# Attention's order respaced, intermediate rows stored for one batch only, and Q and K loaded in transfers to 48, 32 and 16 partitions

## What is computed

```python
qkv = x @ qkv_w.T                      # rotary positions on q and k
outs.append(_sdpa(q[:, :6], k[:, :6], v[:, :6], 1 / sqrt(16)))
# hyperbolic heads:
inner = einsum('bhtd,bhsd->bhts', q, k) - tq * swapaxes(tk, -1, -2)
arg = maximum(-curv * inner, 1 + 1e-7)
scores = 1 / (eps + sqrt(1 / curv) * arccosh(arg)) + causal_bias
outs.append(softmax(scores) @ v)
outs.append(_sdpa(qn, kn, v[:, 10:], sqrt(16)))
x = layernorm(x + concat(outs) @ proj_w.T + proj_b)
# experts: 1024 tokens x top 2 of 8, on the flattened rows
x = layernorm(x + experts(x) + bias)
```

## Time and profile before

| what | value |
|---|---|
| median of 3 runs | 1947.89 us |
| the profiled execution | 1950.01 us, span 1948.4 us |
| projection, 0 to 276 us of the span | 276 us |
| attention, 8 turns, 276 to 1722 us | about 181 us each |
| experts and end | 226 us |
| busy in the span: TensorE, ScalarE, VectorE, GpSimd | 1608.7, 1393.3, 1203.7, 756.2 us |
| DMA, share of 16 engines | 37.5% for the hardware queue, 5.6% for GpSimd's |

### The profile page before, as it was taken

How to read it: one execution, slowest core, us unless ns; L and a number is a source line. 1 busy time by engine, 2 the same in 40 slices (tenths; PEclk the granted TensorE clock), 3 DMA queues, 4 the chain that set the end, 5 groups by cost and what they waited for, 6 DMA issues and landing times.

```text
span 1948.4 us, 38980 instructions
## 1 busy us (share of the span) xinstructions
PE 1608.7 (83%) x13082; PEld 905.8 (46%) x13082; DVE 1203.7 (62%) x3014; ACT 1393.3 (72%) x1460; POOL 756.2 (39%) x369
## 2 busy tenths in 40 slices
PE   7999937876987898789779977986897789779993
PEld 4655612333443344344334433442443344369992
DVE  6877836634766686577657665765785577532234
ACT  2655638896897889788878987897889788851220
POOL 3344333443433444353435434344433465430003
PEclk9999959988997999899889988998998899779997
DMA  4699850255034405510650254054206511358893
GB/s 156 214 242 282 233 154 12 76 87 89 13 50 84 110 2 89 122 34 2 110 122 13 35 96 114 2 73 112 59 2 110 125 34 51 103 195 279 292 338 100
DMA packets 75777, 215.01 MB, mean 110 GB/s; under 512 B 18064, under 2 KB 27664, under 8 KB 69744
## 3 DMA queue, kind: packets, MB, share of 16 engines
q1 hardware_dynamic: 66400, 179.16, 37.5%
q0 software_dynamic: 9200, 33.43, 5.6%
HBM read 143.95 MB, written 68.58 MB: 109 GB/s over the span
## 4 chain that ended last, share of the span: by engine, by line
PE 33%; issue 14%; DVE 9%; ACT 9%; POOL 7%; DMA 5%; SPq 2%; DVEq 0%; POOLq 0%; ACTq 0%
PE a_o L1214 6%; PE a_w L1259 4%; PE a_s L715 4%; PE a_s L727 4%; PE a_s L1199 4%; POOL a_Z L1487 3%; POOL a_R L1484 3%; DVE a_X L1728 2%; PE a_w L1227 2%; PE a_w L1303 2%; DMA K<-t_parts 2%; ACT a_PT L1396 2%; SPq L1120 2%; DMA x_mid<-a_X 2%; ACT a_Z L1414 2%
## 5 line engine op out<-in xcount | busy, mean ns | idle before, releaser
L1396 ACT ACTIVATE a_PT<-a_s 128x1024 f32<-128x1024 f32 (+3 forms) x576 | 460.0, 810 | 154.3 <-PE a_s L1202 94.1
L1487 POOL TENSOR_TENSOR a_Z<-a_Z,a_R 128x2182 f32<-128x2182 f32 x64 | 290.0, 4531 | 449.0 <-ACT a_R L1408 442.2
L1199 PE MATMUL a_s<-Q,K 96*128 96x512 bf16 (+7 forms) x1152 | 330.7, 352 | 103.7 <-ACT a_PT L1396 75.5
L1484 POOL TENSOR_TENSOR a_R<-a_Z 128x2182 f32<-128x2182 f32 x64 | 245.1, 3830 | 242.1 <-DVE a_Z L1600 206.8
L1608 DVE TENSOR_REDUCE a_mx<-a_w 128x1 f32<-128x512 f32 (+2 forms) x576 | 307.3, 550 | 44.0 <-PE a_w L1227 37.7
L1214 PE MATMUL a_o<-a_PT,a_V 128*32 128x512 f32 (+3 forms) x2304 | 271.0, 545 | 74.8 <-ACT a_PT L1396 47.5
L1600 DVE TENSOR_SCALAR_CACHE_REDUCE a_Z<-a_w 128x512 f32<-128x512 f32 (+7 forms) x384 | 202.8, 528 | 116.8 <-PE a_w L1242 69.6
L1259 PE MATMUL a_w<-a_ident,a_R 128*128 128x128 f32 (+1 forms) x1152 | 202.5, 301 | 37.3 <-DVE a_PTh L1654 22.6
L1654 DVE COPY a_PTh<-a_w 128x512 f32<-128x512 f32 (+1 forms) x256 | 158.2, 622 | 102.0 <-PE a_w L1259 100.0
L1227 PE MATMUL a_w<-K,Q 96*128 96x512 bf16 (+2 forms) x576 | 188.8, 334 | 26.4 <-DVE a_mx L1608 10.1
L1199 PEld LDWEIGHTS a_s<-Q,K 99*128 99x128 bf16 (+1 forms) x1152 | 111.4, 103 | 198.8 <-ACT a_PT L1396 105.7
(11 more groups left out here) (166 smaller groups left out, 2539.9 us busy)
## 6 DMA issues: line engine op xcount, KB each, us to landing
qk_parts<-p_parts SPq DMA_DIRECT2D x128, 192.0 KB, 3.4
Q<-in_w SPq DMA_DIRECT2D x46, 512.0 KB, 6.2
K<-in_w SPq DMA_DIRECT2D x46, 512.0 KB, 7.4
Q<-qk_parts SPq DMA_DIRECT2D x144, 128.0 KB, 5.4
K<-qk_parts SPq DMA_DIRECT2D x144, 128.0 KB, 8.1
v_rows<-p_vt SPq DMA_DIRECT2D x8, 2048.0 KB, 9.7
a_V<-v_rows SPq DMA_DIRECT2D x32, 512.0 KB, 9.8
p_xT<-in_xt SPq DMA_DIRECT2D x8, 1024.0 KB, 8.3
```

The lines of the kernel that those rows point to most:

```text
L1199: m = pe.matmul(sB[x % 2][:, i, 0:w], Kb[0:r, h, P * j:P * j + P], Qb[0:r, h, t0:t0 + w], start=True, stop=not diag)
L1396: act.activation(PT[:, u % 2, 2 * k:2 * k + 2, 0:w], sB[x % 2][:, :, 0:w], ACT.Exp, scale=scale_of(GROUPS[g][2 * k])).then_inc(prob.sem, 1)
L1484: pool.tensor_tensor(r, z, z, ALU.mult).then_inc(z_sq.sem, 1)
L1487: pool.tensor_tensor(z, z, r, ALU.add).then_inc(z_sum.sem, 1)
```

## The change

1. **Transfers.** The six pairs are reordered to Q parts 0, 0, 0, 1, 1, 2 and K parts 0, 1, 2, 0, 1, 0. A run of equal Q parts is one transfer whose source is read three times or twice (stride 0), and the K parts of that run are one transfer over three or two parts. So Q and K have transfers of 48, 32 and 16 partitions: 6 for groups 0 and 2, 12 for group 1, and 12 for group 3, of which 6 carry roots into 3, 2 and 1 partitions. The same bytes are moved.
2. **`mid_out`** is executed for batch 0 only. For that, turn 1 stands before the loop on VectorE and GpSimd (code only). For other batches `add_bias` waits for the first layer norm and not for the store.
3. **Order.** The units' `ready` are (13, 35, 51, 66, 87, 102, 118, 135) and were 12, 29, 46, 64, 81, 99, 116, 134; the arguments stand within 6 to 18 quarter steps ahead of it. In the chain `log_distance` and `inverse` come 1 quarter step later, `row_bias` 2, the exponentials 3, 2, 2 and 3, the transposes 6 and 2. The maxima start one step earlier. The late part is respaced and its second layer norm stands 4 to 5 quarter steps earlier. In the final stretch, where late items are mixed into the experts, all that still wait are taken at the last place of the list.

```diff
-QPART = (0, 0, 1, 0, 2, 1)
-KPART = (0, 1, 0, 2, 0, 1)
+PAIRS = ((3, 0), (2, 1), (1, 2))
...
+    def copies(src, n, first, same):
+        if same:
+            return src[first:first + 1].to_broadcast([n, *src.shape[1:]])
+        return src[0:n]
+
+    for qk, buf in enumerate((Qb, Kb)):
+        r = 0
+        for n, part in PAIRS:
+            src = qk_parts[bass.ds(b, 1), qk, :, 2 * BR * block:2 * BR * (block + 1), :]
+            src = src.rearrange("o s (d h) t -> (o s) d h t", d=HD)
             for h0, h1 in runs:
                 i0 = BLOCKS[block].index(h0)
-                found.append((g, buf, r * HD, (r + 1) * HD, (h0, h1, src[:, i0:i0 + h1 - h0, :])))
+                found.append((g, buf, r * HD, (r + n) * HD,
+                              (h0, h1, copies(src[:, :, i0:i0 + h1 - h0, :], n, part, qk == 0))))
...
+        READY = (13, 35, 51, 66, 87, 102, 118, 135)
+        SPREAD = (7, 3, 1, 2, 2, 1, 2, 2)
+        CHAIN = (('square', 0), ('log_square', 4), ('root', 6), ('add_root', 8), ('log_sum', 13), ('log_distance', 16), ('inverse', 18), ('row_bias', 21))
...
-                         (112, ("newton", 0)), (114, ("normalize", 0, 0)), (115, ("normalize", 0, 1)), (116, ("mid_out",)),
-                         (121, ("add_bias",)), (123, ("statistics", 1, 0, NT // 2)), (124, ("statistics", 1, NT // 2, NT)),
...
                 elif kind == "mid_out":
-                    rows_out(d, x_mid, 0, mid_sent)
+                    if is_routed(d):
+                        rows_out(d, x_mid, 0, mid_sent)
...
                 elif kind == "add_bias":
-                    dve.wait_ge(mid_sent.sem, mid_sent.at(d))
+                    if is_routed(d):
+                        dve.wait_ge(mid_sent.sem, mid_sent.at(d))
+                    else:
+                        dve.wait_ge(normed.sem, normed.at(d, 0))
```

More of the change, by code:

```diff
@@ L32 @@
 GW = P // HD
-QPART = (0, 0, 1, 0, 2, 1)
-KPART = (0, 1, 0, 2, 0, 1)
-NPAIR = len(QPART)
+PAIRS = ((3, 0), (2, 1), (1, 2))
+NPAIR = sum(n for n, _ in PAIRS)
 KR = NPAIR * HD
@@ L598, in head_loads @@
     found, block = [], BLOCK_OF[g]
[L599 to L602, removed]
+    def copies(src, n, first, same):
[7 more added lines that the diff above has]
+            src = src.rearrange("o s (d h) t -> (o s) d h t", d=HD)
             for h0, h1 in runs:
                 i0 = BLOCKS[block].index(h0)
-                found.append((g, buf, r * HD, (r + 1) * HD, (h0, h1, src[:, i0:i0 + h1 - h0, :])))
[L606 to L610, removed]
+                found.append((g, buf, r * HD, (r + n) * HD,
+                              (h0, h1, copies(src[:, :, i0:i0 + h1 - h0, :], n, part, qk == 0))))
+            if g == 3:
+                src = t_parts[bass.ds(b, 1), :, qk * N_HYP:(qk + 1) * N_HYP, :].rearrange("o s h t -> (o s) h t")
+                found.append((g, buf, KR + r, KR + r + n, (HYP0, COS0, copies(src, n, part, qk == 0))))
+            r += n
     return found
@@ L921, in put @@
             work[at // NSLOT][at % NSLOT].append(item)
-        for n in range(NU):
-            ready = LEAD + SPAN * n // (NU - 1)
+        READY = (13, 35, 51, 66, 87, 102, 118, 135)
+        SPREAD = (7, 3, 1, 2, 2, 1, 2, 2)
+        CHAIN = (('square', 0), ('log_square', 4), ('root', 6), ('add_root', 8), ('log_sum', 13), ('log_distance', 16), ('inverse', 18), ('row_bias', 21))
+        for n, ready in enumerate(READY):
             args = [("argument", n, k, pc) for k, seg in enumerate(segments(n)) for pc in range(len(seg[3]))]
-            span = 2 * len(args) if n else 8
+            span = SPREAD[n] * len(args) if n else SPREAD[n]
             for a, item in enumerate(args):
                 put(ready - span + a * span // len(args), item)
[L929 to L939, removed]
+            for kind, at in CHAIN:
+                put(ready + at, (kind, n))
+            for k, at in enumerate((23, 24, 26, 29)):
+                put(ready + at, ("hyp_exp", n, k))
+            for part, at in enumerate((33, 34)):
                 for q in range(len(turns(n, part))):
-                    put(ready + turned + q, ("turn", n, part, q))
+                    put(ready + at + q, ("turn", n, part, q))
             if n % 2:
@@ L959, in columns_of @@
             return hs[0] * NT, (hs[-1] + 1) * NT
[L961 removed]
+        SUMS = {0: 119, 1: 121, 2: 143, 5: 149, 6: 155, 7: 163, 3: 178, 4: 179}
+        ROWS, PROJECT, STATISTICS = (40, 46, 54, 63, 71, 80, 86, 94), (42, 52, 55, 64, 77, 84, 91, 95), (48, 53, 61, 71, 81, 86, 94, 97)
         for n, at in SUMS.items():
             put(at, ("turn_sums", n))
[L964 removed]
+        put(40, ("unstage",))
         for k, n in enumerate(SUMS):
[L966 to L969, removed]
[L970 to L973 removed]
+            put(ROWS[k], ("turn_rows", n))
+            put(PROJECT[k], ("project", n))
+            put(STATISTICS[k], ("statistics", 0, n, n + 1))
+        for at, item in ((25, ("shift",)), (104, ("variance", 0)), (106, ("inverse_root", 0)), (112, ("newton", 0)), (114, ("normalize", 0, 0)), (115, ("normalize", 0, 1)), (116, ("mid_out",)), (117, ("add_bias",)), (118, ("statistics", 1, 0, NT // 2)), (119, ("statistics", 1, NT // 2, NT)), (120, ("variance", 1)), (121, ("inverse_root", 1)), (124, ("newton", 1)), (126, ("normalize", 1, 0)), (128, ("normalize", 1, 1)), (128, ("rows_out",)), (136, ("rows_in",))):
             put(at, item)
@@ L987, in attend, with is_routed @@
                 "rows_out", "shift")
+        def is_routed(d):
+            return isinstance(d, int) and d == 0
         def is_late(item):
@@ L1012, in attend @@
                 finish += [("second", t - 1), ("y_copy", t - 1)]
-            take = SIZES[t] if t < len(SIZES) else 0
+            take = SIZES[t] if t < len(SIZES) - 1 else len(waiting)
             finish, waiting = finish + waiting[:take], waiting[take:]
@@ L1556, in _ @@
             pool.wait_ge(others, 16 * NOTHER)
-            with nc.Fori(1, B - 1, engines=[pool.engine], hint_back_edge=True) as b:
+            turn(1)
+            with nc.Fori(2, B - 1, engines=[pool.engine], hint_back_edge=True) as b:
                 turn(b)
@@ L1769, in _ @@
             dve.wait_ge(others, 16 * NOTHER)
-            with nc.Fori(1, B, engines=[dve.engine], hint_back_edge=True) as b:
+            turn(1)
+            with nc.Fori(2, B, engines=[dve.engine], hint_back_edge=True) as b:
                 turn(b)
```

7 lines of the change are left out of this document (3 added, 4 removed).

## The result

The changed kernel took **2099.27 us** (median of 4 runs, 2087.64 to 2104.90), the kernel before 1948.43 beside it: ratio 1.0751, 95% interval 1.0711 to 1.079. The profiled execution took 2087.64 us. It is slower, as forecast, but by 151 us by the medians (137.6 between the profiled executions) where 58 were forecast, and above the range.

The account below looks back on a forecast made before the run. Attention was taken as bound by TensorE and ScalarE waiting for each other, projection by TensorE. 42 + 47 + 16 - 24 - 9 - 14 = +58 on 1950.0 gave 2008, less 2.1 above the median: 2006 us, range 1930 to 2050.

Parts of the forecast that it names:

- How many engines: Loads of Q and K: transfers to 48 and 32 partitions use 3 and 2 DMA engines, not 16.
- the bracket `<-DMA K<-t_parts`: Sign in the profile after: a wait of about 9 us at the first argument of every turn.
- the four late p_xT: Sign in projection: waits for p_xT, the batch's input, of 5 to 17 us in four batches.
- Projection +42: Projection: loads issued ahead crowd the first engine and delay the next batch's input; +42 us, bounds +21 and +54.
- "28.2 us" from last to first argument: Between turns' arguments: the load of `heads(3)` sets 28.2 us; six stretches, average 20.4 before, give +47, bounds +31 and +62.
- The first transition, "0": First stretch from last to first argument: 28.1 us already, so no change, 0.
- Restart at the low clock +16: Turn after the wait on TensorE: slower after waiting, 6 x 2.7 = +16 us (0 to +32).
- The store -24: Dropped store of x_mid: VectorE's sum with the bias no longer waits for it, -24 us (0 to -24).
- Respacing and the quarter step -23: Attention turn: stretched chain and respacing -14 us (-49 to +14); one quarter step less between first and last argument -9.
- The layer norm beside GpSimd, "0": Layer norm on VectorE: its hold beside GpSimd leaves the first, returns at the second; 0 (-25 to +9).
- Rival A: Loads of Q and K: split over sixteen engines by the 48 partitions written, -71, 1877 us; chance 0.14.
- "1965 to 2045": Whole kernel: span in us given to the forecast case alone, said to span the terms' bounds.

Follow-up runs that it names:

- e6: The changed kernel, with SyncE waiting for the landing of `heads(3)` before it issues `heads(2)`: 2075.63 us.
- e7: The changed kernel, with `out` and the load of X moving one eighth of their bytes from the second turn on: 2070.85 us.
- e9: The changed kernel with both edits, the wait of e6 and the cut of `out` and X of e7: 2036.40 us.
- e1_order: The changed kernel's order and dropped store of x_mid, with the 16-partition transfers of the kernel before: 1965.82 us.
- e5_order_wait: e1_order, with SyncE waiting for the landing of `heads(3)` before it issues `heads(2)`: 1922.28 us.
- e3_sixteen: The changed kernel, same pieces into 48, 32 and 16 partitions, but with the 16 rows of a head as outermost count: 1902.36 us.
- e11: The kernel before, without the store of x_mid in turns 1 to 7 and nothing else changed: 1952.74 us.
- e2: The kernel before, with the changed kernel's new transfers (`PAIRS` and `head_loads`) alone: 2161.37 us.
- e14: The kernel before, with the transfers of e3_sixteen and without the store of x_mid in turns 1 to 7: 1930.67 us.

## Why the prediction was wrong in size

**How many engines: right.** 3 engines for 48 partitions: the share is 19.0% and a row takes 0.34 us. This reading carried the direction. Right too were the bracket `<-DMA K<-t_parts` in every turn and the one x_mid wait left. The bracket was to be about 9 us and was 18. Of the four late p_xT, forecast at 5 to 17 us, two came at 19 and 16 us, one at 4 and one at 0.3.

**Projection +42: right**, +46.

**"28.2 us" from last to first argument: the term that failed.** It was 38.5 in the mean of the last six, and 37.5 in the first turn, where I had written 0. Six were short by 10.3 us each and the first by 9.4: 71 us, which is the whole miss of 69 in this row (my 20.4 for before's six was 20.7). The measured +116 also lies above the upper bound of this term, +62. Its parts, for one of the six stretches, by the runs:
- `heads(2)` beside it: 3.2 us (e6). The sum had nothing for what is issued behind the load.
- `out` and X: 2.7 us for seven eighths of their bytes, thus 3.1 in all (e7), where 2.6 stood for X, and nothing for `out`.
- Both together took off 8.0 (e9, 38.5 to 30.5), 2.1 more than their sum: each seems to hide a part of the other.
- What is left is 30.5 against the 25.6 that my sum gives without X: the row of 0.33 us, taken from one row on a quiet chip, holds only in the calm (0.32); at the start of a load it is 0.45. The first row came 1.5 to 4.5 us after its issue (4.5 behind `out`), not 1, and in e6 and e9 the argument starts 0.6 us after the last row.

So the mechanism was right and a price from one idle moment was multiplied by 72.

**The first transition, "0": wrong for the same reason.** What held it was most likely `heads(2)` beside it: e1_order has 27.2 us there, e5_order_wait 22.2, with X issued 5.3 us after the last argument in both. In the kernel before X comes 5.1 us after it there and 13.6 to 16.6 in the other six, so the same meeting is likely; it wasn't tried in that kernel. Few engines came on top.

**Restart at the low clock +16: right in size.** The changed kernel's stretches from first to last argument sum to 20 us more than those of e3_sixteen, with the same order and no wait. The first argument takes 0.62 and not 0.40 us there, as in the earlier trace rows. During the wait (1258:1297) the granted clock is 0.71 of 2.4 GHz, and in the 10 us behind it 0.75; in the 10 us behind e3_sixteen's first argument at 1157.74 it is 1.00. Not all of the 20 us need be the clock: the second turn alone is 6.8 us longer, and in it VectorE waits 10.0 us for x_mid, where e3_sixteen has 5.2.

**The store -24: wrong alone, and more with the slow transfers.** By itself -2 (e11, not to be told from none). I took the whole wait without asking what VectorE would meet next, though the earlier trace rows had shown the hold. In e2 VectorE's wait for the store was 8.6 us in the mean of six turns (3.4 to 3.7 in before), and its removal brought 39 us.

**Respacing and the quarter step -23: about right.** -28 in the stretches, -21 by the ratios (e14 to e3). How much of it is the quarter step, the chain or the late part was not tried alone.

**The layer norm beside GpSimd, "0": right.** The hold left the first layer norm and came back beside L1490 in five of seven turns, at the second half of the second layer norm and not the first. Timeline of the changed kernel, DVE and then POOL:

```profile
1446.95 1.37 DVE L1733 TENSOR_SCALAR a_X<-a_X,a_mv,a_rs 128x256 f32<-128x256 f32 x4
1448.87 5.91 DVE L1733 TENSOR_SCALAR a_X<-a_X,a_mv,a_rs 128x256 f32<-128x256 f32 x4
```
```profile
1449.34 4.97 POOL L1490 TENSOR_TENSOR a_Z<-a_Z,a_R 128x2182 f32<-128x2182 f32 x1 [6.77 <-ACT a_R L1411]
```

In the other two turns these four take 1.37 us, and L1490, which begins 0.5 us after them, takes 5.6 us and not 5.0 (1251.64 and 1252.11 is one of them). Over the whole span the layer norms' 128 instructions are busy for 66.6 us, and were for 68.5.

**Rival A** (sixteen engines, 1877 us) was told apart rightly by the maxima's packets. Made true in e3_sixteen, it gives 1902: the stretch is 21.2 and not 18.6 us (18 us in seven).

**The range was too narrow by its own terms.** "1965 to 2045" is said to span the bounds above, but the bounds of all terms add up to 1893 at the low end and 2110 at the high one, and no reason is given for the narrower span.

## What to carry to other kernels

Ask for each transfer what its outermost count is, on both sides. Here, merging three loads into one that has 3 outermost took thirteen engines away, and turning the same loop inside out gave them back. A price for a piece, read where the chip is quiet, is a lower bound: take a second one from where other transfers run. A wait that is removed is a gain only if the next instruction meets nothing, above all on VectorE beside GpSimd.

## What the runs showed of the hardware

- A row of 8 KB took 0.32 us with two or three engines running and nothing else, 0.45 at the start of a load, 0.64 with sixteen engines writing 48 and 32 partitions (65.5 us in 102 rows, 210 GB/s), and 0.79 (e1_order) to 0.93 (16 x 8192 bytes x 1.03 / 145 GB/s) with sixteen writing 16 partitions.
- In e1_order the same load ended 21.7 us after the last argument in one turn and 28.5 in another. In the second one the next load was issued 1 us earlier, and `out` and X 2 and 5.5 us earlier. With that next load held back, all seven took 21.7 to 23.5 us (e5). The load's end is a chain of single-partition transfers in one engine's line, which the next load joins.
- An instruction of 0.17 us on VectorE took 4.18 us beside a GpSimd sum of 4.80 us that had begun 0.64 us earlier (e11), and both ended together.
